# Relation sums in a graph network: bits turned into numbers in their own buffer, in one ring of eight instead of rings of two and four

## The reference, cut to what matters

```python
def _rgcn_layer(x, W, W_root, b, src, dst, edge_type, num_nodes, num_rel):
    h = jnp.einsum('nd,rdf->rnf', x, W)
    msg = h[edge_type, src]
    comb = dst * num_rel + edge_type
    cnt = jax.ops.segment_sum(jnp.ones(src.shape, dtype=x.dtype), comb, num_segments=num_nodes * num_rel)
    norm = 1.0 / jnp.clip(cnt[comb], 1.0)
    agg = jax.ops.segment_sum(msg * norm[:, None], dst, num_segments=num_nodes)
    return agg + x @ W_root + b
...
for l in range(weight.shape[0]):
    x = _rgcn_layer(x, weight[l], root[l], bias[l], src, dst, edge_type, num_nodes, num_rel)
```

## Time and profile before

| | us |
|---|---|
| median of 3 runs | 5897.77 (5896.78 to 5898.04) |
| the profiled execution, its own time | 5894.55 |
| its span (first to last instruction) | 5892.6 |
| first `relation_sums`, from the first cut to the last finish | 4720.30 to 5244.0 |
| second `relation_sums`, the same | 5333.9 to 5857.6 |

### The profile page before, as it was taken

The page is one execution under the profiler, slowest core; times in us unless marked ns, Lnnn a source line. Parts: engine busy times, 40 slices in busy tenths (PEclk is TensorE's granted clock), DMA queues, the critical chain, the costliest instruction groups (busy, mean ns, idle before and its releaser), DMA issues. The chain is left out here.

```text
span 5892.6 us, 107675 instructions
## 1 busy us (share of the span) xinstructions
PE 4004.4 (68%) x31282; PEld 3016.9 (51%) x31283; DVE 3825.4 (65%) x9916; ACT 2230.1 (38%) x2892; POOL 1396.0 (24%) x1703
## 2 busy tenths in 40 slices
PE   4666676635445554445558888888888788878886
PEld 2222276624444444444444444444444488867886
DVE  7999967755655555656534555535555677767776
ACT  2444332001111111111115655545555466646664
POOL 0000000037777777777740000000000000000000
PEclk8999988855555555555558999979999799978998
DMA  1111144522222222222111111111111111111110
GB/s 45 58 67 56 65 175 171 215 61 59 59 59 59 59 59 58 64 58 54 48 33 62 56 56 57 49 51 56 56 56 56 51 46 44 39 36 61 39 44 23
DMA packets 235223, 370.66 MB, mean 63 GB/s; under 512 B 169839, under 2 KB 175973, under 8 KB 235142
## 3 DMA queue, kind: packets, MB, share of 16 engines
q1 hardware_dynamic: 190006, 264.11, 13.8%
q0 software_dynamic: 41536, 85.08, 5.4%
q10 hardware_dynamic: 3600, 20.48, 0.8%
HBM read 292.58 MB, written 76.99 MB: 63 GB/s over the span
## 5 line engine op out<-in xcount | busy, mean ns | idle before, releaser
L1069 POOL DMA_INDIRECT en_got<-edge_q,en_now x1296 | 1302.1, 1005 | 409.4 <-issue 325.1
L1258 PE MATMUL en_t<-ident,en_got 128*128 128x128 f32 x1296 | 361.4, 435 | 957.7 <-DVE en_got L1152 957.7
L1296 ACT ACTIVATE en_hid<-en_t 128x512 f32<-128x512 f32 x324 | 193.5, 597 | 1649.6 <-DMA en_got<-edge_q,en_now 1408.2
L1258 PEld LDWEIGHTS en_t<-ident,en_got 128*128 128x128 f32 x1296 | 231.9, 217 | 1036.1 <-DVE en_got L1152 1036.1
L1266 PEld LDWEIGHTS en_o<-en_w2s,en_hid 128*128 128x128 f32 x2592 | 583.0, 334 | 0.0
L1266 PE MATMUL en_o<-en_w2s,en_hid 128*128 128x64 f32 x2592 | 577.6, 411 | 0.0
L1152 DVE TENSOR_TENSOR en_got<-en_got,p (+1 forms) x324 | 224.5, 693 | 494.7 <-ACTq L1290 462.4
L1855 PE MATMUL r1s_ps<-hp,r1s_count 128*128 128x193 bf16 x5000 | 445.8, 253 | 81.2 <-DVE r1s_count L1807 57.0
L1855 PE MATMUL r0s_ps<-hp,r0s_count 128*128 128x193 bf16 x5000 | 445.6, 253 | 81.4 <-DVE r0s_count L1807 56.2
L456 PE MATMUL cnt_ps<-cnt_hot_l,cnt_hot_k 128*128 128x400 bf16 x1600 | 359.6, 356 | 193.9 <-DVE cnt_hot_l L421 182.0
L1855 PEld LDWEIGHTS r1s_ps<-hp,r1s_count 128*128 128x128 bf16 x5000 | 432.4, 100 | 94.5 <-issue 91.1
(11 more groups left out here) (393 smaller groups left out, 7633.3 us busy)
## 6 DMA issues: line engine op xcount, KB each, us to landing
en_got<-edge_q,en_now POOLq DMA_INDIRECT x1296
count_panels<-cnt_panel SPq DMA_DIRECT2D x25, 800.0 KB, 3.4
type_panels<-cnt_panel SPq DMA_DIRECT2D x25, 800.0 KB, 4.8
c0s_panel<-count_panels SPq DMA_DIRECT2D x25, 800.0 KB, 4.3
count_rows<-c0s_rows ACTq DMA_DIRECT2D x25, 800.0 KB, 3.5
c1s_panel<-count_panels SPq DMA_DIRECT2D x25, 800.0 KB, 5.5
c1s_rows<-count_rows SPq DMA_DIRECT2D x25, 800.0 KB, 7.3
en_raw<-count_panels SPq DMA_DIRECT2D x25, 800.0 KB
```

The lines of the kernel that those rows point to most:

```text
L1069: pool.indirect_dma_start(out=got[:, i, j, :], out_offset=None, in_=k.q[:, :], in_offset=bass.IndirectOffsetOnAxis(ap=now[i][:, j:j + 1], ...
L1258: last = pe.transpose(tps[i % 2][:, j * P:(j + 1) * P], got[:, i, j, :], k.ident[:, :])
L1296: act.activation(hid[i % 2][:, :], tps[i % 2][:, :], ACT.Relu).then_inc(lined, 1)
```

## The change: what it does

The `count` buffers go. There are eight buffers `bits`, one for each relation, and the number is written over the bits that it is made of: `count[r]` is the same memory, read as bf16. `cut_out` of relation r no longer waits for the number of relation r-2, but for TensorE to be done with relation r of the window before (`used`, which now starts at 8). VectorE's and ScalarE's conversions keep the wait for their bits and lose the wait for `used`. The buffers of the ring take 8 x 6400 bytes of a partition in place of 6 x 6400.

```diff
-        CUTS, RING = 2, 4
...
-        bits = [sb(f"bits{u}", [P, W, P], U16) for u in range(CUTS)]
-        count = [sb(f"count{u}", [P, W, P], BF16) for u in range(RING)]
+        bits = [sb(f"bits{r}", [P, W, P], U16) for r in range(NREL)]
+        count = [b[:, :, :].bitcast(BF16) for b in bits]
...
             def cut_out(w, u, r):
-                if r >= CUTS:
-                    made(v, w, r - CUTS, 0)
-                elif not (isinstance(w, int) and w == 0):
-                    made(v, w - 1, r - CUTS + NREL, 0)
-                v.tensor_scalar(bits[r % CUTS][:, :, :], packed[u][:, :, :], 2 * r, 3,
+                wait_alone(v, used, w * NREL + (r + 1), passed[0])
+                v.tensor_scalar(bits[r][:, :, :], packed[u][:, :, :], 2 * r, 3,
                                 ALU.logical_shift_right, ALU.bitwise_and).then_inc(cut, 1)
 
             def number(w, r):
                 wait_alone(v, cut, w * NREL + (r + 1 + 2 * NREL), passed[0])
-                wait_alone(v, used, w * NREL + (r + 1), passed[0])
-                v.tensor_copy(count[r % RING][:, :, :], bits[r % CUTS][:, :, :]).then_inc(made_v, 1)
+                v.tensor_copy(count[r], bits[r][:, :, :]).then_inc(made_v, 1)
 
             def finish(w, u, begun):
                 own.at(begun)
-                wait_alone(v, used, w * NREL + (NREL + RING), passed[0])
+                wait_alone(v, used, w * NREL + 2 * NREL, passed[0])
...
                 for r in BY_A:
                     act.wait_ge(cut, w * NREL + (r + 1 + 2 * NREL))
-                    act.wait_ge(used, w * NREL + (r + 1))
-                    act.activation(count[r % RING][:, :, :], bits[r % CUTS][:, :, :], ACT.Copy).then_inc(made_a, 1)
+                    act.activation(count[r], bits[r][:, :, :], ACT.Copy).then_inc(made_a, 1)
...
-            pe.sem_inc(used, RING)
+            pe.sem_inc(used, NREL)
...
-                        last = pe.matmul(ps[u][:, r * 2 * P:r * 2 * P + 3 * D + 1], count[r % RING][:, b, :],
+                        last = pe.matmul(ps[u][:, r * 2 * P:r * 2 * P + 3 * D + 1], count[r][:, b, :],
```

## The result

The changed kernel takes 5739.9 us (median of 4 runs, 5733.2 to 5743.8) against 5897.3 (4 runs, 5890.7 to 5898.0): a ratio of 0.9734, 95% interval 0.972 to 0.9748. The forecast was 5742. The profiled execution took 5738.8 with a span of 5736.5, against 5894.6 and 5892.6.

The account below looks back on a forecast made before the run. VectorE and ScalarE waiting for each other was taken as the bound. Two stages, each 78.0 us shorter, bring 5894.55 to 5738.6; with the median 3.2 above, 5742 us, range 5709 to 5790 (about 0.85).

Parts of the forecast that it names:

- The loop between VectorE and ScalarE over two bits buffers: Relation sums before: cuts wait for ScalarE's numbers and VectorE's casts, 4.8 us of a 20.62 us window.
- The path that sets the window: Relation sums after: finish, cuts of relations 4 and 5, cast of 4, then matmuls of relations 4 to 7: 17.35 us.
- the finish: VectorE's block closing a window, between the cuts of relations 3 and 4, taken as 5.76 us.
- The tie with ScalarE's relation 5: ScalarE's side, through relation 5's conversion and three relations of matmuls, also gives 17.35 us, so no slack there.
- Its length: Forecast window of each relation sum after the change: 17.35 us, against 20.62 before.
- the 78.0 forecast: Saving in us expected from each of the two relation sums, last finish of the first at 5160.5 instead of 5238.4.
- The total: Whole kernel: 5894.55 - 156.0 = 5738.6 us for the profiled execution, median 3.2 above, so 5742.
- the lower bound: VectorE's cast over its own source: 0.985 us as now, of bounds 0.985 and 3.49; ScalarE's added cost taken as 0.
- The clock, the rival with 0.09: TensorE's clock falls in the relation sums, up to 1.66 us lost a window: 5757 to 5822 us, chance 0.09.
- the same three gaps in each window: Clock rival's reading of TensorE before: gaps of about 2.5, 0.47 and 0.47 us, at clock 1.00 and 0.91 alike.
- relations 0 to 3 come back in time: Cuts' new wait for TensorE: those buffers are free by 8.64 us into a window, wanted from 11.53 on.
- TensorE's 0.69 us: TensorE's expected idle time ahead of relation 4 in each window, above its floor of 16.66 us.

Follow-up runs that it names:

- rings of four and four: Kernel before with four bits buffers in place of two, its four count buffers kept, conversions not in place: 5750.1 us, ratio 0.975.
- ring of four in place: Changed kernel with four bits buffers in place of eight, conversions still over their source: 5784.9 us (one run).
- full multiplication: Changed kernel with one more VectorE multiplication a window, 128 x 1536 f32, right behind the finish: 5881.6 us (one run).

## Why the prediction was right, point by point

- **What bounded the kernel.** The loop between VectorE and ScalarE over two bits buffers: shown. Four more count buffers left it alone, two more bits buffers removed it.
- **The path that sets the window.** Shown on three sides: one more instruction on it lengthens the window, off it not; the finish one place later takes the gap away, one place earlier widens it. The tie with ScalarE's relation 5 is in the rows too: from 5011.28 its number is ready 3.02 later, at 5014.30, and TensorE comes to it at 5012.29 + 2.08 = 5014.37. In the steady part the profile puts every gap down to VectorE's cast.
- **Its length.** 17.35 forecast, 17.40 measured. The term that was mis-sized is the finish: 5.80 in place of 5.76, since its reduction takes 2831 ns in the mean where the window read for the sum had 2.79 us (2800 ns in the mean of that stage); why it takes longer is not shown. 24 x 0.05 = 1.2 us a stage is what separates the 78.0 forecast from the 76.8 measured.
- **The total.** 5742 forecast, 5739.9 measured. So close a hit is luck in part: the 2.4 us that the two stages fell short of the forecast were made up, but for 0.2, by code that did not change, and the median stands 1.2 above the profiled execution where the forecast added 3.2.
- **In place at no cost.** 984 ns against 985, 2857 against 2864: the lower bound was the right one. With conversions that are not in place and the same window (rings of four and four) they take 987 and 2858. What the Trainium skill lists for VectorE's fastest mode ("VectorE: DVE Perf Modes", section "What auto-detection actually checks") is 16-bit elements, step one, a single source and both operands in SBUF, the on-chip memory, and not that source and target differ. The trace agrees with that: 984 ns in place.
- **The clock, the rival with 0.09.** It did not come with a gap of 0.56 us as the profile counts it, and stayed away with 1.35 and with the 1.47 of the ring of four in place. But it was a real danger: the kernel with the full multiplication had gaps of 2.13 to 2.16 us, and there it came in 21 of 24 windows and cost 1.65 us in each. One reading in the rival was wrong: the kernel before did not have the same three gaps in each window. Over nearly all of the 160 us at 0.91 it had a single one of some 2.15 us, as in this row:

```profile
5104.29 18.48 PE L1855 MATMUL r0s_ps<-hp,r0s_count 128*128 128x193 bf16 x200 [2.15 <-DVE r0s_count L1807]
```

So the rows nearest to the forecast, with one gap a window, were those at the lower clock, and what was left against the rival was that the gap would be 0.69 us and not 2.15. The Trainium skill tells of short idle times between groups of matmuls that make the clock swing ("TensorE: Matmul & The Clock Gate", section "A second HAM failure mode: psum-queue depth-cycling"). The trace of the full multiplication agrees with that (0.91 to 0.93), the one of this kernel, at 1.00 with 0.56 us, does not.

- **Four of the new ring's eight buffers** carry most of the gain already (18.29 us with four in place, 2.3 of the 3.2 us a window); the prediction had only said that relations 0 to 3 come back in time, and with eight they do.

What the change left on the table stood in the prediction's sum as TensorE's 0.69 us: it is taken by moving the finish behind the cast of relation 4, for 5708.3 us. Then TensorE runs the two stages without a break at full clock, so a further gain there would need fewer or shorter matmuls.

## What to carry to other kernels

Ask of each buffer which wait it closes before adding any: two more bits buffers were worth 3.2 us a window, four more count buffers none. When a loop of waits is opened, write down the next path from its first release to its last and look at what stands on it without need; here an instruction block of 5.8 us stood one place too early, and the same move cost time before the rings were deep enough. A delay on an engine that feeds TensorE can cost twice, once as itself and once as the lower clock behind a longer gap, so a lengthened path should be sized with both.

## What the runs showed of the hardware

- A 16-bit cast on VectorE and a conversion on ScalarE over their own source cost what they cost into another buffer (984 against 985 ns, 2857 against 2864 ns for 128 x 3200).
- An additional 1.57 us on the feeding engine cost 3.22 us in 21 of 24 windows and 1.57 in the other three; 0.81 us cost 0.78 in each (18.18 against 17.40). The gaps were 2.1 and 1.35 us, the granted clock 0.91 to 0.93 and 1.00.
- The length of a gap alone does not tell. The kernel before had gaps of 2.5, 0.47 and 0.47 us in each of ten windows with the clock at 1.00, and, once the clock had fallen, a single one of 2.15 in each of seven with it at 0.91. With the finish ahead of cut 3 each window had a gap of 3.7 us, and the clock fell in 12 of 24.
- Unchanged code ahead of the stage ended up to 18 us apart from kernel to kernel (one profiled execution each), so small effects have to be read from the stage and not from the total.
